# Two Mamba layers on one core: TensorE starts each forward sum with D*xs, ScalarE copies the sum out

## The reference, cut to what matters

```python
x = silu(causal_conv(x, conv_w) + conv_b)           # called xs in the kernel
proj = x @ W_x;  dt, Bm, Cm = split(proj)
dt = softplus(dt @ W_dt + b_dt);  A = -exp(A_log)
for t in tokens:                                     # 192 channels x 16 states
    h = exp(dt[t] * A) * h + dt[t] * x[t] * Bm[t]
    y[t] = sum over the 16 states of h * Cm[t]
y = y + x * D                                        # the skip term, D*xs
out = (y * silu(z)) @ W_out                          # layer 1: out_fwd + out_bwd
```

## Time and profile before

| | |
|---|---|
| median of three runs | 2136.84 us |
| profiled execution, its own time | 2136.97 us |
| its span | 2135.0 us |
| granted TensorE clock, mean | 0.939 |
| DVE, POOL, ACT busy | 1829.8, 1938.6, 1162.8 us |
| PE matmuls busy | 1814.8 us |

### The profile page before, as it was taken

How to read it: one execution, slowest core, us unless ns; L and a number is a source line. 1 busy time by engine, 2 the same in 40 slices (tenths; PEclk the granted TensorE clock), 3 DMA queues, 4 the chain that set the end, 5 groups by cost and what they waited for, 6 DMA issues and landing times. The chain is left out here.

```text
span 2135.0 us, 16128 instructions
## 1 busy us (share of the span) xinstructions
PE 1814.8 (85%) x4474; PEld 705.1 (33%) x4474; DVE 1829.8 (86%) x1110; ACT 1162.8 (54%) x1206; POOL 1938.6 (91%) x852
## 2 busy tenths in 40 slices
PE   5797789897898899789889879879979878977777
PEld 2232233332333333233333333323334323333232
DVE  2888887876899988997799997998889998899994
ACT  2756465655746645645656745745575564453331
POOL 0998999897898999998999999899899999999996
PEclk9799999998999899999899989999999999988997
DMA  3567466555575866675665785685566576677673
GB/s 83 206 211 187 154 226 184 172 183 196 148 222 193 213 188 238 190 200 203 201 173 205 234 208 202 199 213 186 187 188 207 203 206 193 238 208 203 222 211 90
DMA packets 124454, 415.01 MB, mean 194 GB/s; under 512 B 18556, under 2 KB 22924, under 8 KB 124364
## 3 DMA queue, kind: packets, MB, share of 16 engines
q1 hardware_dynamic: 124364, 413.98, 64.1%
HBM read 403.48 MB, written 6.29 MB: 192 GB/s over the span
## 5 line engine op out<-in xcount | busy, mean ns | idle before, releaser
L861 POOL TENSOR_TENSOR ring<-ring,c_ring 128x1024 f32<-128x1024 f32 x576 | 1346.0, 2363 | 89.8 <-DVE ring L817 66.6
L495 PE MATMUL y_ps<-ring,wp 128*128 128x512 f32 x2304 | 1179.2, 629 | 53.8 <-DVE yv_fwd L797 26.8
L817 DVE TENSOR_TENSOR_SCAN ring<-a_ring,b_ps 128x1024 f32<-128x1024 f32 x392 | 895.5, 2284 | 33.2 <-ACT a_ring L624 2.3
L495 PEld LDWEIGHTS y_ps<-ring,wp 128*128 128x128 f32 x2304 | 452.2, 200 | 540.4 <-issue 418.4
L817 DVE TENSOR_TENSOR_SCAN ring<-b_ps,b_ring 128x1024 f32<-128x1024 f32 x184 | 417.1, 2274 | 64.9 <-POOL b_ring L855 31.3
L624 ACT ACTIVATE a_ring<-delta_ab,wp 128x1024 f32<-128x1024 f32 x240 | 271.8, 1140 | 183.7 <-DVE ring L817 183.2
L855 POOL TENSOR_TENSOR b_ring<-u_ab,b_ring 128x1024 f32<-128x1024 f32 x144 | 341.0, 2368 | 28.5 <-DMA b_ring<-b_rows 28.3
L784 DVE TENSOR_TENSOR b_ps<-u_ab,b_ps 128x1024 f32<-128x1024 f32 x240 | 291.0, 1213 | 87.7 <-PE b_ps L483 81.4
L617 ACT ACT_TABLE_LOAD x186 | 238.6, 1283 | 90.8 <-PE bank L518 37.5
L624 ACT ACTIVATE b_ps<-delta_ab,wp 128x1024 f32<-128x1024 f32 x144 | 160.4, 1115 | 213.0 <-DVE ring L817 212.6
L624 ACT ACTIVATE a_ring<-delta_m,wp 128x1024 f32<-128x1024 f32 x152 | 173.6, 1143 | 155.0 <-DVE ring L817 154.7
(11 more groups left out here) (75 smaller groups left out, 958.9 us busy)
## 6 DMA issues: line engine op xcount, KB each, us to landing
c_ring<-c_rows SPq DMA_DIRECT2D x384, 512.0 KB, 5.0
c_ring<-c_rows SPq DMA_DIRECT2D x384, 256.0 KB, 4.3
b_ring<-b_rows SPq DMA_DIRECT2D x144, 512.0 KB, 5.2
b_ring<-b_rows SPq DMA_DIRECT2D x80, 256.0 KB, 5.2
out<-io SPq DMA_DIRECT2D x16, 192.0 KB, 4.9
io<-x SPq DMA_DIRECT2D x6, 384.0 KB, 6.7
b_in<-parts SPq DMA_DIRECT2D x36, 64.0 KB, 2.1
dt_in<-parts SPq DMA_DIRECT2D x72, 24.0 KB
```

The costliest lines, as they stand in the source:

```text
L495: nc.tensor.matmul(half(y_ps[:, :], j), ident, half(ring[:, g % RING, :], j), start=(n == 0), stop=(n == NS - 1)).then_inc(g_summed, 1)
L817: nc.vector.tensor_tensor_scan(out=h, data0=a, data1=b, initial=0.0, op0=ALU.mult, op1=ALU.add).then_inc(h_ready, 1)
L861: nc.gpsimd.tensor_tensor(r, r, c_ring[:, g % C_RING, :], ALU.mult).then_inc(g_ready, 1)
```

## The change

For fwd items alone, three things are changed. TensorE adds D*xs itself: at the first product of a tile it first multiplies the half of yv by the identity into y_ps (start=True), and then adds the product. VectorE's `take` returns without doing anything. ScalarE gets a phase "take" ahead of its look-ahead phases: at the fifth step of the next tile it waits for the first half of the finished sum, copies it into yv, waits for the second half and copies that. The takes of rows and bwd items stay on VectorE.

```diff
-ACT_ORDER = ("ahead_a2", "ahead_a", "jobs")
+ACT_ORDER = ("take", "ahead_a2", "ahead_a", "jobs")
...
+                if kind == FWD and n == 0:
+                    pe.wait_ge(K["skip_done"][kind], 3 * pair + k + 1)
+                    nc.tensor.matmul(half(y_ps[:, :], j), ident, half(yv_of(kind, pair, k), j), start=True, stop=False)
                 nc.tensor.matmul(half(y_ps[:, :], j), ident, half(ring[:, g % RING, :], j),
-                                 start=(n == 0), stop=(n == NS - 1)).then_inc(g_summed, 1)
+                                 start=(n == 0 and kind != FWD), stop=(n == NS - 1)).then_inc(g_summed, 1)
...
+            def take_forward(g):
+                if g % NS != SUM_LAG or g < NS or ITEMS[(g - NS) // STEPS]["kind"] != FWD:
+                    return
+                tile = g // NS - 1
+                it = ITEMS[tile // TILES]
+                for j in range(2):
+                    act.wait_ge(g_summed, 2 * NS * (tile + 1) - 1 + j)
+                    nc.scalar.activation(half(yv_of(FWD, it["pair"], tile % TILES), j), half(y_ps[:, :], j), ACT.Copy).then_inc(y_taken, 1)
+
+            walk(ACT_ORDER, job, ahead_a=look_ahead, ahead_a2=look_ahead_psum, take=take_forward)
...
                 kind, pair, k = it["kind"], it["pair"], tile % TILES
-                if j == 0:
-                    if kind != BWD:
-                        dve.wait_ge(K["skip_done"][kind], 3 * pair + k + 1)
-                    if kind == BWD:
-                        dve.wait_ge(y_taken, 2 * (tile - TILES + 1))
+                if kind == FWD:
+                    return
+                if j == 0 and kind == ROWS:
+                    dve.wait_ge(K["skip_done"][kind], 3 * pair + k + 1)
+                elif j == 0:
+                    dve.wait_ge(y_taken, 2 * (tile - TILES + 1))
                 dve.wait_ge(g_summed, 2 * NS * (tile + 1) - 1 + j)
```

More of the change, by code:

```diff
@@ L717, in job @@
                                          bias=ln[0:C, 3:4]).then_inc(affine_done, 1)
-            walk(ACT_ORDER, job, ahead_a=look_ahead, ahead_a2=look_ahead_psum)
+            def take_forward(g):
[7 more added lines that the diff above has]
+            walk(ACT_ORDER, job, ahead_a=look_ahead, ahead_a2=look_ahead_psum, take=take_forward)
         @block.vector
```

## The result

The change makes the kernel slower. The median is 2151.4 us of four runs (2147.46 to 2153.7) against 2136.32 us of four runs of the kernel before on the same chip (2130.63 to 2139.29): a ratio of 1.0076, with a 95% interval of 1.0062 to 1.0091. The profiled execution took 2150.5 us (span 2148.5), 13.5 more than that of before. The forecast was 2146.5 us, in a range from 2133 to 2157. One run of all those in this document, 2381.5 us long at a granted clock of 0.74, is left out of the medians.

The account below looks back on a forecast made before the run. No single engine bounds the kernel: TensorE is full in an item's first tiles, VectorE in fwd 1.2. Terms 8.1 + 4.0 + 0.7 + 0 - 0.8 - 2.5 = +9.5 us gave 2146.5 us, range 2133 to 2157.

Parts of the forecast that it names:

- Term 1: s4 of bwd 0, 1, 2: ScalarE's waiting second copy delays the silu and TensorE's convolution, 3 x 2.7 = +8.1 us.
- Term 2: s4 of the four fwd items: two new matmuls where TensorE is full, 3 x 0.9 + 1.3 = +4.0 us.
- Term 3: s20 of fwd 0: the first new matmul makes a job that ScalarE needs 1.5 us late, +0.7 us.
- Term 4: s20 of fwd 1, 2, 3: VectorE's gain is lost at a later wait for DMA, 0 us.
- Term 5: s36 of all four fwd items: VectorE's saving mostly goes into waiting for the row of B, 4 x 0.2 = -0.8 us.
- Term 6: s4 of bwd 3: VectorE saves two half takes and a 1.65 us wait for B, POOL limits it, -2.5 us.
- The signs that the prediction set itself: Bwd .0 tiles grow from 55 to 57.5 us; wrong if unchanged, or if fwd .1 and .2 change over 1 us.
- The losses are hidden: Rival, chance 0.22: VectorE and POOL hold bwd .0 too, so terms 1 and 2 shrink; +2.4, 2139 us.
- The copies hold back decays at s20 and s36: Rival, chance 0.15: late decays make fwd .1 and .2 matmuls cost 8 x 1.5 = +12 more, 2158.6 us.
- Faster: Rival, chance 0.09: VectorE's takes hold the chain, 13.9 us come back, 2123 us; convolution at s4 of bwd starts no later.

Follow-up runs that it names:

- the padded kernel: Three half-width zero-weight matmuls added on TensorE at s4 of bwd 0 to 2, ahead of the waiting convolution, against the changed kernel; 2147.01 us, one run.

## Why the forecast came out

Slower was right. The size came out short: +9.5 us were forecast, and +13.5 are measured in the profile and +15.1 by the medians. Most steps held; two sizes, one sign and one reason did not. That the sum lies this near is in part luck: measured less forecast is +3.6 in term 1, +0.4, -1.9, +2.1 and +2.8 in terms 2 to 5, -0.5 in term 6 and -2.4 in tiles that had no term. The signs that the prediction set itself came out mixed. The new wait of 2.84 us and the longer bwd tiles are there; but fwd .1 and .2 changing by more than 1 us was to be a sign against it, and in this profile all four .1 tiles (by -1.2 to +2.1) and fwd 3.2 did. In the two other profiles of the kernel fwd 2.1 (+1.1 and +1.25) and fwd 3.2 did.

**Term 1, s4 of bwd 0, 1, 2: the mechanism right, the size too small.** Forecast +8.1, measured +11.7. Each link is in the rows: the second copy waits for the half sum that the convolution of s3 stands ahead of, the silu comes late, and TensorE waits 2.84 us (forecast "about 2.9"). bwd 0.0 has +2.68, the 2.7 of the working. What was missing is the clock: behind a wait of 2.84 us it fell to 1.2 GHz in bwd 1.0 and 2.0, which the padded kernel shows to be 1.7 us each. The other 0.3, in bwd 2.0 alone, stays there with the padding. The upper bound of this term, 10.5, had another reason (the silu behind) and was still too low. The Trainium skill (PSUM — Partial Sum Buffer, Engine vs sequencer instructions) has ScalarE's queue as strictly first in, first out; the trace agrees: the decay starts 2.94 us behind the first copy (1126.57 to 1129.51) where the waiting copy stands between them, and 0.50 us behind it (1123.56 to 1124.06) in the kernel with the second copy late.

**Term 2, s4 of the fwd items: right.** Forecast 3 x 0.9 + 1.3 = +4.0, measured 0.95 + 0.86 + 0.87 + 1.72 = +4.4, and much the same in the kernel with the matmuls alone. Two of these tiles were 1.3 us longer in one other profile each (fwd 1.0 and fwd 0.0), so the +4.4 is not a fixed number. In fwd 0.0 POOL hid nothing, and both matmuls are paid in full. The rows of fwd 1.0 show the one matmul that has cover (the old 0.82 of the earlier trace rows is gone) and the one behind the convolution that has none:

```profile
949.22 1.02 PE L497 MATMUL y_ps<-yv_fwd,wp 128*128 128x512 f32 x2
...
950.93 1.88 PE L545 MATMUL bank<-x,w_conv 96*128 96x512 f32 x4
952.65 1.02 PE L497 MATMUL y_ps<-yv_fwd,wp 128*128 128x512 f32 x2
```

**Term 3, s20 of fwd 0: the wrong sign.** Forecast +0.7, measured -1.2 (-0.6 and -0.8 in the two other profiles of the same kernel; the kernel before moved by +0.5 by itself). The job behind the new matmul is late by 1.5 us, as worked out: it starts 2.79 us behind the row of B at 495.52, where it was 1.30 behind that at 494.40. Before and now:

```profile
494.40 0.60 PE L483 MATMUL b_ps<-b_in,sel 96*128 96x512 bf16 x2
...
495.70 1.02 PE L518 MATMUL bank<-scratch,wp 96*96 96x512 f32 x2
...
503.25 1.99 PE L518 MATMUL bank<-scratch,wp 96*96 96x512 f32 x2 [2.52 <-DVE parts L839]
```
```profile
495.52 0.60 PE L483 MATMUL b_ps<-b_in,sel 96*128 96x512 bf16 x2
...
498.31 1.02 PE L521 MATMUL bank<-scratch,wp 96*96 96x512 f32 x2
...
505.33 1.07 PE L521 MATMUL bank<-scratch,wp 96*96 96x512 f32 x2 [1.27 <-DVE parts L852]
```

But the next job waits for VectorE's "parts" anyway. That wait was 2.52 us before and is 1.27 now: there was slack that the working did not look for. The clock gives something back too. Behind the longer wait of before it was at half (0.50 from 503.10 to 506.40), and the job and the addition behind it took 3.35 us up to the next row of B at 506.60; now it stays at 1.00, and they take 1.77 (505.33 to 507.10). How much of the 1.2 us comes from this is not shown: with the copies alone the clock is at half there too, from 509.96, and the tile is 1.08 shorter.

**Term 4, s20 of fwd 1, 2, 3: within what can be told.** Forecast 0. The three tiles are -1.02, +2.05 and +1.03, but fwd 2.1 moves by +1.5 without any change.

**Term 5, s36: right three times, wrong once.** Forecast -0.2 each, for the reason that VectorE saves the take and then waits for the row of B; the trace has that wait (0.81 us), the tiles are -0.09, -0.09 and -0.08, and without the new matmuls two of them give back 1.0. The fourth, fwd 3.2, is +2.26 (+2.07 and +2.39 in the repetitions). TensorE waits 2.64 us for the copies here, where it is 1.65 in the three others, and its clock is at half while it makes the new matmuls:

```profile
1930.60 2.04 PE L497 MATMUL y_ps<-yv_rows,wp 128*128 128x512 f32 x2 [2.64 <-issue]
1932.44 1.91 PE L498 MATMUL y_ps<-ring,wp 128*128 128x512 f32 x2
...
1936.74 0.60 PE L483 MATMUL b_ps<-b_in,sel_m 96*128 96x512 bf16 x2
```
```profile
1930.60:1936.60 6.00, 6.00 (x8) 2.45 (x9) 3.60 (x3) 3.61 (x4) 6.00 (x4) 0.56 1.01 243
```
```profile
1937.45 1.23 DVE L796 TENSOR_TENSOR b_ps<-u_m,b_ps 128x1024 f32<-128x1024 f32 x1 [3.16 <-PE b_ps L483]
```

The two new matmuls and the two additions take 6.1 us (1930.60 to 1936.74), where four times 0.86 us at full clock would be 3.4, and VectorE waits 3.16 us for the row of B behind them. TensorE's wait has "issue" in place of a releaser; that it is for the copies is read from ScalarE's order (decay from 1928.87, copies from 1929.92):

```profile
1929.92 1.06 ACT L729 ACTIVATE yv_rows<-y_ps 128x512 f32<-128x512 f32 x2
```

The half clock is not new at this place. Before the change it was there as well, without the two matmuls in it:

```profile
1916.20:1922.90 6.70, 6.04 (x8) 2.48 (x9) 6.52 (x5) 3.30 (x3) 6.70 (x4) 0.50 0.92 212
```

The kernel of the zero weights has the same instructions here as the changed one, and in its profile the clock was back at full speed sooner. The same four take 5.17 us (1927.46 to 1932.63), VectorE's wait is 2.18, and the tile is +1.29: 0.97 or 0.98 us less each time.

```profile
1933.33 1.23 DVE L804 TENSOR_TENSOR b_ps<-u_m,b_ps 128x1024 f32<-128x1024 f32 x1 [2.18 <-PE b_ps L485]
```

So some 1.0 of the 2.3 us is the clock's at the least. Where VectorE takes at s36 and TensorE makes the same new matmuls, the wait is 1.15 us and the tile unchanged; with the copies and no matmuls it is 0.44 shorter. So both halves of the change are needed for this loss. How the rest divides into wait, matmuls and clock was not measured.

**Term 6, s4 of bwd 3: the number right, one of its reasons not.** Forecast -2.5, measured -2.99, and -2.74 to -3.00 in the six other kernels with these copies. VectorE's wait of 1.65 us is gone:

```profile
1989.06 1.21 DVE L796 TENSOR_TENSOR b_ps<-u_ab,b_ps 128x1024 f32<-128x1024 f32 x1
```

The working laid that wait on the take. The kernel with the matmuls alone has the take at its old place on VectorE, and TensorE still waits for it, 1.31 and 1.68 us; yet VectorE's wait is gone there as well, and the tile is 1.99 shorter. What differs is the clock. The same six rows behind the take, before and with the matmuls alone, took:

```profile
1968.59 5.46 PE L495 MATMUL y_ps<-ring,wp 128*128 128x512 f32 x6 [1.68 <-DVE yv_rows L797]
```
```profile
1971.15 2.81 PE L498 MATMUL y_ps<-ring,wp 128*128 128x512 f32 x6 [1.68 <-DVE yv_rows L809]
```

The granted clock was 0.50 from 1967.40 to 1974.10 before, behind waits of 2.97 and 1.68 us, and 1.00 from 1968.10 to 1975.30 there. So by this one profile about 2 us of the gain can be had with the takes where they were, if the clock does not fall, and about 1 us, near the 1.16 of the two half takes, came only with the copies.

**The rivals.** "The losses are hidden" fails: no POOL or VectorE hid any of the 2.7. "The copies hold back decays at s20 and s36" fails in fwd 0.1, 1.1 and three of the .2 tiles; fwd 3.2 is a cousin of it, though through TensorE. "Faster" fails at its own point: the convolution of s4 starts later. The kernel with the matmuls alone shows that the other half of its argument was not absurd, since TensorE's 20.6 us cost only 1.9 us there.

**What the two halves cost together.** Alone they measure 1.0009 and 1.0025, times 2135 us some 1.9 and 5.3 us; together 1.0076 on one chip and 1.0092 on another, 16 and 20 us. Two places of this are in the profiles: at s36 the copies alone change the four tiles by +0.69, -1.00, -0.99 and -0.44, the matmuls alone by about 0, and both by +2.0 in all (3.7 us more than the parts); and at bwd 3.0 both claim the same time, -1.99 for the one, -2.99 for the other, -2.99 together. That is 5.7 us of the 9 to 12 by which the whole exceeds the parts. The rest, 3 to 7, stays open; each of these ratios is sure to some 3 or 4 us only, so it may be scatter.

## What to carry to other kernels

An instruction that is moved to an idle engine takes its wait with it. Ask what stands behind it in that engine's order and who waits for that, before asking how busy the engine is: here two copies of 0.6 us cost up to 4.7 us a place, and with the second of them behind the silus the place cost 0.2 to 0.4. Price a new wait of TensorE with the slower clock that can follow it, and look for the half clock that is in the profile already, since a change can move it either way. Apply such a change only at the places where the profile shows the gain: one tile of twelve gave a faster kernel than all twelve.

## What the runs showed of the hardware

- TensorE's granted clock was 1.00 up to and through a wait of 2.84 us and could be at half, 1.2 GHz, behind it. It fell in bwd 1.0 and 2.0 in all three profiles of the changed kernel and never in bwd 0.0; with the copies alone (one profile) it fell in 0.0 and 2.0 and not in 1.0. Behind waits of 1.83 us it stayed, at three places of three. Why one wait of 2.84 us is punished and its twin is not, while the changed kernel has the same pattern in three profiles, was not worked out.
- A fall cost the tile 1.7 us where TensorE was the bound, and the clock was back at 1.00 by 1138, 5.3 us behind the start of the convolution.
- Three matmuls with zero weights, 2.6 us of useless work, kept the clock at 1.00 at three places of three and made the tiles 1.7 us shorter at two.
- The half clock moved other terms as well. Behind waits of 2.97 and 1.68 us in bwd 3.0 of the kernel before, six rows of additions took 5.46 us at 0.50, and 2.81 at 1.00 in the kernel with the matmuls alone. In fwd 3.2 four small matmuls took 6.1 us in one kernel and 5.2 in another with the same instructions there.
